# Row maxima taken in pairs: one reduction over two neighbouring PSUM banks, and one such pair of banks

## The reference, cut to what matters

```python
Q = (decoder_input @ W_q).reshape(B, Sd, HEADS, HEAD_DIM)
K = (encoder_output @ W_k).reshape(B, Se, HEADS, HEAD_DIM)
scores = jnp.einsum('bqhd,bkhd->bhqk', Q, K) / jnp.sqrt(jnp.float32(HEAD_DIM))
attn = jax.nn.softmax(scores, axis=-1)          # each of 512 rows over 512 keys
out = jnp.einsum('bhqk,bkhd->bqhd', attn, V).reshape(B, Sd, E)
```

## Time and profile before

| what | value |
|---|---|
| median of 3 runs | 685.81 us (685.5 to 687.59) |
| the profiled execution | 689.51 us, of which 687.3 us are the span of the trace |
| busy: PE, DVE, ACT, POOL | 552.0, 439.9, 304.7, 162.4 us |
| maximum tiles: DVE reductions | 256, 170.4 us busy, mean 682 ns |
| maximum tiles: matmuls | 256, mean 409 ns |
| mean granted TensorE clock | 0.877 of full speed |

### The profile page before, as it was taken

One profiled execution on the slowest core, in us unless ns is written; L12 is line 12 of the kernel. 1 busy time (PEld: TensorE's weight loads), 2 busy tenths in 40 slices (PEclk: granted clock), 3 DMA queues, 4 the chain that ended last, 5 costly groups with the idle time before them and its releaser, 6 DMA issues. The chain is left out here.

```text
span 687.3 us, 6312 instructions
## 1 busy us (share of the span) xinstructions
PE 552.0 (80%) x1928; PEld 207.6 (30%) x1928; DVE 439.9 (64%) x675; ACT 304.7 (44%) x509; POOL 162.4 (24%) x177
## 2 busy tenths in 40 slices
PE   4287786878987799999798998888988787886662
PEld 1111132213333221334342223534413343330531
DVE  3279429894537789746769897477666556624224
ACT  2320252221655537363667554354765525665031
POOL 0035425541212233413113342321100010000000
PEclk9778898995999999999999999898979978976666
DMA  4710034260223221122113102001111200000000
GB/s 140 200 32 0 1 46 123 81 134 1 46 32 100 72 76 46 48 47 31 59 46 113 39 9 78 31 17 55 56 60 48 77 0 2 1 2 0 31 0 31
DMA packets 34354, 34.52 MB, mean 50 GB/s; under 512 B 5713, under 2 KB 32017, under 8 KB 34321
## 3 DMA queue, kind: packets, MB, share of 16 engines
q1 hardware_dynamic: 33504, 33.92, 18.3%
q10 hardware_dynamic: 816, 0.20, 0.1%
HBM read 22.37 MB, written 8.39 MB: 45 GB/s over the span
## 5 line engine op out<-in xcount | busy, mean ns | idle before, releaser
L954 DVE TENSOR_REDUCE MX<-bank 128x1 f32<-128x512 f32 x256 | 170.4, 682 | 128.0 <-PE bank L444 127.6
L754 ACT ACTIVATE PT<-bank 128x512 f32<-128x512 f32 x256 | 147.4, 595 | 168.2 <-PE bank L453 159.6
L444 PE MATMUL bank<-KS,QS 96*128 96x512 bf16 x256 | 102.4, 409 | 27.9 <-DVE MX L954 24.1
L1014 POOL TENSOR_TENSOR Pq<-qT,St 128x512 f32<-128x512 f32 x64 | 84.0, 1313 | 159.0 <-DVE St L863 140.0
L453 PE MATMUL bank<-QS,KS 99*128 99x512 bf16 x256 | 103.8, 412 | 19.3 <-ACT PT L754 12.2
L863 DVE TENSOR_TENSOR_SCAN St<-ab,U 128x512 f32<-128x512 f32 x64 | 91.3, 1426 | 1.0
L429 PE MATMUL bank<-Pq,hsel 128*32 128x512 f32 x128 | 75.2, 673 | 13.5 <-POOL Pq L1014 13.1
L467 PE MATMUL bank<-PT,Vs 128*32 128x512 f32 x512 | 78.0, 671 | 0.8 <-ACT PT L754 0.8
L453 PEld LDWEIGHTS bank<-QS,KS 99*128 99x128 bf16 x256 | 25.1, 100 | 111.8 <-issue 61.7
L444 PEld LDWEIGHTS bank<-KS,QS 96*128 96x128 bf16 x256 | 25.4, 100 | 100.6 <-DVE MX L954 57.6
L857 DVE TENSOR_TENSOR U<-kT,bank 128x512 f32<-128x512 f32 x64 | 42.9, 671 | 15.8 <-PE bank L422 15.7
(11 more groups left out here) (119 smaller groups left out, 666.7 us busy)
## 6 DMA issues: line engine op xcount, KB each, us to landing
KS<-k_parts SPq DMA_DIRECT2D x96, 64.0 KB, 2.3
QS<-q_parts SPq DMA_DIRECT2D x96, 64.0 KB, 2.3
VB<-parts SPq DMA_DIRECT2D x24, 128.0 KB
k_parts<-parts SPq DMA_DIRECT2D x12, 256.0 KB, 2.1
q_parts<-parts SPq DMA_DIRECT2D x12, 256.0 KB, 2.3
xT<-in_xT SPq DMA_DIRECT2D x4, 512.0 KB, 3.4
cT<-in_cT SPq DMA_DIRECT2D x4, 512.0 KB, 3.3
xtok<-in_x SPq DMA_DIRECT2D x4, 512.0 KB, 3.9
```

Source lines behind the costliest of these rows:

```text
L444: pe.matmul(bank(n)[:, :], QS[0:NS, h, i * P:(i + 1) * P], KS[0:NS, h, :], start=True, stop=True).then_inc(filled(n), 1)
L754: act.activation(PT[:, n % 2, j, :], bank(name)[:, :], ACT.Exp).then_inc(emptied(name), 1)
L954: dve.tensor_reduce(MX[:, NT * h + i:NT * h + i + 1], bank(n)[:, :], AX.X, ALU.max).then_inc(emptied(n), 1)
L1014: pool.tensor_tensor(Pq[:, e % 2, :], qT[:, :], St[:, e % 2, :], ALU.mult).then_inc(p_done, 1)
```

## The change

A maximum tile becomes a pair of tiles. Two neighbouring banks, the old banks 3 and 4, become one tensor `maxima` of 1024 columns with one pair of semaphores, those of bank 3. PE waits once, writes two matmuls of 512 columns into its halves and signals after the second. DVE waits once and reduces both halves in one instruction of 2x512 elements into two columns of MX. The table deals out pairs: 22 over the same 40 quarters and 10 over the same 20, 128 pairs in all. The mr tiles use the first half of the same tensor, under the same semaphores.

```diff
-    _tiles = [(_h, _i) for _h in _heads for _i in range(NT)]
+    _tiles = [(_h, _i) for _h in _heads for _i in range(NT // 2)]
...
-                for which, h, tile in MAXIMA.get((n, i), []):
-                    use(f"m{h}.{tile}", stage[which], 3 + tile % 2)
+                for which, h, half in MAXIMA.get((n, i), []):
+                    use(f"m{h}.{half}", stage[which], 3)
...
+        maxima = ps("maxima", 2)
+        banks = [maxima[:, 0:512] if i == 3 else None if i == 4 else ps(f"bank{i}", 1) for i in range(8)]
...
-            def max_tile(b, h, i):
-                if h % 4 == 0 and i == 0:
+            def max_pair(b, h, half):
+                if h % 4 == 0 and half == 0:
                     pe.wait_ge(K_in[h // 4], count(96, b, 96))
                     pe.wait_ge(Q_in[h // 4], count(96, b, 96))
-                n = f"m{h}.{i}"
+                n = f"m{h}.{half}"
                 pe.wait_ge(*free_for(n, b))
-                pe.matmul(bank(n)[:, :], QS[0:NS, h, i * P:(i + 1) * P], KS[0:NS, h, :],
-                          start=True, stop=True).then_inc(filled(n), 1)
+                for i in range(2):
+                    at = (2 * half + i) * P
+                    ins = pe.matmul(maxima[:, 512 * i:512 * i + 512], QS[0:NS, h, at:at + P], KS[0:NS, h, :],
+                                    start=True, stop=True)
+                ins.then_inc(filled(n), 1)
...
-                dve.tensor_reduce(MX[:, NT * h + i:NT * h + i + 1], bank(n)[:, :], AX.X, ALU.max).then_inc(emptied(n), 1)
+                at = NT * h + 2 * half
+                dve.tensor_reduce(MX[:, at:at + 2], maxima[:, :].rearrange("p (t n) -> p t n", t=2),
+                                  AX.X, ALU.max).then_inc(emptied(n), 1)
...
-                pool.wait_ge(*read(f"m{4 * g + 3}.{NT - 2}", b))
-                pool.wait_ge(*read(f"m{4 * g + 3}.{NT - 1}", b))
+                pool.wait_ge(*read(f"m{4 * g + 3}.1", b))
```

More of the change, by code:

```diff
@@ L150, in sem, with ps @@
             return counting[-1]
-        banks = [ctx.enter_context(nc.psum_tensor(f"bank{i}", [P, 512], F32)) for i in range(8)]
+        def ps(name, n):
+            return ctx.enter_context(nc.psum_tensor(name, [P, 512 * n], F32))
+        maxima = ps("maxima", 2)
+        banks = [maxima[:, 0:512] if i == 3 else None if i == 4 else ps(f"bank{i}", 1) for i in range(8)]
         full = [sem(f"bank{i}_full") for i in range(8)]
@@ L576, in _ @@
                             by_token(f"V{i}", b, cT, xwv, i)
-                        for which, h, tile in MAXIMA.get((n, i), []):
+                        for which, h, half in MAXIMA.get((n, i), []):
                             if stage[which] is not None:
-                                max_tile(stage[which], h, tile)
+                                max_pair(stage[which], h, half)
                         if (n, i) in ROWS and stage[ROWS[n, i][0]] is not None:
```

## The result

| | before | pairs |
|---|---|---|
| first comparison, median | 686.70 us (4 runs) | 729.35 us (4 runs) |
| ratio, 95% interval | | 1.053 (1.041 to 1.065) |
| second comparison, another chip, median | 687.51 us (17 runs) | 724.22 us (6 runs) |
| ratio, 95% interval | | 1.041 (1.033 to 1.048) |
| profiled execution, its span | 689.51, 687.3 us | 727.88, 725.7 us |

The kernel is slower, as forecast, but by 28 to 36 us and not by 14; the times lie above the range of 685 to 712. The ratios leave out disturbed executions, in which a kernel is over 1.5% above its own fastest; the medians do not, which is why they lie further apart than the ratios.

The account below looks back on a forecast made before the run. PE was taken as nearest to a bound, with DVE mostly following it. The terms 12.8 + 3.6 - 2 gave +14.4 us, so 685.8 became 700.2, rounded to 699; range 691 to 711 (0.68), 8 in 10 within 685 to 712.

Parts of the forecast that it names:

- first term: PE at mr, directly behind the pair just issued in 15 places of 16: 18.4 us less 5.6 given back, +12.8 us.
- The wait at each mr: From a pair's second matmul to mr on PE: 0.42 + 1.22 + 0.14 = 1.78 us; 18.4 us added in all.
- One pair in flight: PE must wait until the whole pair is read: twelve close pairs lose 7 us, 3.4 us of waits go, +3.6 us.
- the rest: Recurrences, where DVE saves 0.07 us for each pair, and POOL's parts, whose later start is hidden: -2 us, ends -6 and +4.
- I assume that half of the 15 stalls meet one such wait: PE's later waits, 0.7 us on average, shrink after a stall at mr: 8 x 0.7 = 5.6 us given back.
- The reduction's listed time: DVE's maxima: a pair reduction takes 1.22 us against 1.364 for two, so listed busy time falls by 18 us over 128 pairs.
- The saved fixed cost: Rival: DVE's saving reaches the path at PE's waits for the maxima, without loss at mr: 674 to 682 us, chance 0.13.
- The wash: Rival: stalls at mr are absorbed as DVE and ACT catch up and PE's later waits go: 684 to 688 us, chance 0.10.
- The third: Rival: the single pair of banks bounds everywhere, 0.2 us for each of 128 pairs, 25 us: 715 to 725 us, chance 0.09.

Follow-up runs that it names:

- experiment 3: Only mr0 to mr2 moved to side banks: in the changed kernel 690.20 us (1.003), in the kernel before 683.30 (0.990), beside 689.55; two further kernels 696.51 and 692.06.

## Why the prediction was right or wrong

**The mechanism** of the first term was right: no throughput on DVE, and mr behind the pair just issued. The order and one bank number decide it, as experiment 3 shows. It is not the whole loss, and the sum was 14.4 us where 26 are measured at equal clock and 28 to 36 by the ratios.

**The wait at each mr** was right to the hundredth at mr1 (1.78 us). The sum of 18.4 us was 22.8. mr1 was priced from batch 0 alone, "batches differ little"; in batches 2 and 3, where a norm of the feed-forward stage (L844) stands ahead on DVE, the excess was 3.55 and 2.56 us and not 1.56, so mr1 made 9.0 and not 6.2. In batch 2:

```profile
477.75 3.29 DVE L844 TENSOR_SCALAR x<-x1b,mv,rs 128x256 f32<-128x256 f32 x4 [0.40 <-POOL rs L1013]
478.33 0.60 PE L450 MATMUL maxima<-KS,QS 96*128 96x512 bf16 x2
480.96 1.21 DVE L962 TENSOR_REDUCE MX<-maxima 128x2 f32<-128x1024 f32 x1
482.32 0.26 PE L439 MATMUL maxima<-identb,MP 128*128 128x128 bf16 x1 [3.39 <-DVE MX L962]
```

mr0 was taken at 3.6 and added 5.4.

**One pair in flight and the rest**, +3.6 and -2 in the sum, are the step that failed by most. Together they were priced at +1.6 us, and the two kernels without a stall at mr differ by 9 (5 to 13). The least distance of 1.91 us was right (1.93), and so was the reduction's 1.22 us (1.218); what was too small is what the single pair of banks costs over the whole run. PE's waits at the maxima and for L925, where 7 us were to come and 3.4 to go, are together 9 us longer in the pairs.

**"I assume that half of the 15 stalls meet one such wait"**, the 5.6 us to be given back: the 0.7 us have rows behind them and the half has none, but the runs do not speak against the size. 22.8 us of stall and 9 us for the pairs make 32, and 26 are measured, so some 6 us were given back (2 to 10 with the interval above). The waits say where: at the maxima PE waits 31.5 and 32.2 us in the pair kernels without stalls at mr, 28.8 with those of mr3 alone and 27.9 with all of them; for POOL's product it is 13.9 and 15.1 us without and 11.2 with all. The three stalls of mr3, 4.7 us, cost nothing that shows. Those of mr0, mr1 and mr2 cost close to their length: 23 us of stall, 21 us at equal clock. With single tiles, 14.9 us cost 16 and 5.4 taken away brought 6. That the size came out near 5.6 is luck, since the half was a guess and nearly all of it lies at mr3.

**The clock** is missing from the sum. The changed kernel is granted 0.858 to 0.897 where the one before has 0.889 in the median, which adds from 0 to 17 us to one execution and 2 to 10 to the ratios.

**The reduction's listed time** was to fall by 18 us: 256 at 682 ns less 128 at 1218 ns are 18.7. The busy time fell by 14.5, as neighbours had overlapped.

**The rivals.** The saved fixed cost brought nothing that shows: with the stalls away, pairs are 1.3% slower than tiles. The wash, in which the stalls are given back, came only for a small part. The third, pairs late in ordinary quarters with 715 to 725 us, met the time of the second comparison (724), and by luck: it priced the pairs at 25 us and left the stalls at mr as they were, and the pairs cost 9. PE waited at 29 of 128 pairs, not at more than half.

## What to carry to other kernels

When buffers are merged, list everything else that shares their semaphore, and for each such user name the instruction that it now waits for; here one small transpose in the same bank cost 4 to 5%, and another bank number gives it back. Price a stall of the fullest engine near its full length, unless a row shows a later wait that it shortens: here 23 us cost 21 and only the 5 us of mr3 were free. Give the kernel before the same side gain before judging the change by itself: against the kernel as it was the pairs looked 0.3% slower, against the kernel with the same banks 1.3%. A bank that a rare user borrows from a busy double buffer is worth moving even where the waits look small: 5.4 us of excess, mostly 0.6 to 1.1 us at a time, were 1%.

## What the runs showed of the hardware

The same instructions took 712.0 to 729.5 us, with 146 to 207 us at the lower clock level, 0.31 us for each of these; most of the spread inside a comparison went with the clock. Two 512-column reductions back to back and one of 2x512 differ by 0.07 us in a trace (1.29 and 1.22), and the reduction over two neighbouring PSUM banks, 1218 ns for 1024 columns, took what another DVE operation of 1024 elements took before (1219 ns).
